# A perceiver block with a mixture of experts on one core: the clears of the dispatch buffer one at a time, and two blocks' weights behind the rows

## The reference

```python
x = x + xattn(layernorm(x), ctx, ctx)    # 16 heads, queries from x, keys and values from ctx
x = x + mamba(layernorm(x))              # see below
x = x + moe(layernorm(x))

# mamba: project to 1024 channels, conv of 4 taps, silu, then for each of 16 states
h = exp(delta_t * A) * h + delta_t * B_t * x_t
y_t = sum_over_states(h * C_t) + D * x_t

# moe: 16 experts, grouped routing (2 of 4 groups, then 4 experts a token)
act = silu(x @ gate.T) * (x @ up.T)      # 512 -> 256
y = sum_over_chosen(weight * (act @ down.T))
```

## Time and profile before

| | |
|---|---|
| runs | 1340.01, 1334.44, 1340.54 us; median 1340.01 |
| profiled execution | 1334.18 us, of which the span of the trace is 1332.2 |
| busy share of the span | PE 86%, DVE 66%, ACT 47%, POOL 10% |
| DMA | 266.27 MB, mean 200 GB/s; 58.20 MB of it in POOL's queue |
| clears | 38 of 1024 KB and 2 of 768 KB, issued from 84.9 to 312.4 us |

### The profile page before, as it was taken

The page is one execution under the profiler, slowest core; times in us unless marked ns, Lnnn a source line. Parts: engine busy times, 40 slices in busy tenths (PEclk is TensorE's granted clock), DMA queues, the critical chain, the costliest instruction groups (busy, mean ns, idle before and its releaser), DMA issues.

```text
span 1332.2 us, 13289 instructions
## 1 busy us (share of the span) xinstructions
PE 1143.1 (86%) x4276; PEld 729.0 (55%) x4276; DVE 881.5 (66%) x946; ACT 621.5 (47%) x1366; POOL 134.0 (10%) x113
## 2 busy tenths in 40 slices
PE   6988769789797899998889989629999999999992
PEld 4875646566564567675557757324444445444451
DVE  1311579666757999967799995877999974224312
ACT  4542665435355655537556635624455422222321
POOL 0010003201000043000007000030000000233002
PEclk9998889989998999999899999759999998999997
DMA  8375006998601145340035331068999984999994
GB/s 281 111 245 194 4 17 221 404 396 326 223 9 16 33 125 175 78 145 0 17 72 150 119 123 44 0 225 274 360 357 351 375 316 152 375 357 406 410 382 126
DMA packets 115188, 266.27 MB, mean 200 GB/s; under 512 B 11280, under 2 KB 44208, under 8 KB 115120
## 3 DMA queue, kind: packets, MB, share of 16 engines
q1 hardware_dynamic: 99248, 207.22, 45.1%
q0 software_dynamic: 15872, 58.20, 11.1%
HBM read 197.07 MB, written 68.32 MB: 199 GB/s over the span
## 4 chain that ended last, share of the span: by engine, by line
PE 46%; DVE 35%; DMA 8%; ACT 7%; issue 3%; POOL 1%; SPq 0%; POOLq 0%; DVEq 0%; ACTq 0%
DVE state L1348 12%; PE bank L815 9%; PE bank L776 7%; DVE state L1345 6%; PE bank L683 5%; PE bank L695 4%; PE bank L836 4%; PE bank L716 4%; DVE decay L1352 3%; DMA ctx<-in_ctx_t 3%; DVE state L1355 3%; DVE y_acc L1359 2%; PE bank L632 2%; DMA bc_bcast<-bc_scratch 2%; PE bank L747 2%
## 5 line engine op out<-in xcount | busy, mean ns | idle before, releaser
L1348 DVE TENSOR_TENSOR_SCAN state<-decay,state 128x2048 f32<-128x2048 f32 x64 | 282.9, 4421 | 23.5 <-ACT decay L1102 22.6
L815 PE MATMUL bank<-expert_w,block_x_t 128*128 128x512 f32 x496 | 227.0, 601 | 1.8 <-ACT block_x_t L1154 1.7
L683 PE MATMUL bank<-decay,params 128*128 128x512 f32 x384 | 173.3, 595 | 5.9 <-DVE decay L1352 5.9
L1639 POOL DMA_INDIRECT dispatched<-ffn_x,slot x32 | 73.0, 2280 | 756.3 <-DVE slot L1441 747.7
L1102 ACT ACTIVATE decay<-delta_even,params 128x256 f32<-128x256 f32 x256 | 107.2, 498 | 82.7 <-PE bank L683 74.2
L815 PEld LDWEIGHTS bank<-expert_w,block_x_t 128*128 128x128 f32 x496 | 91.6, 195 | 93.7 <-issue 91.6
L695 PE MATMUL bank<-ctx,queries_ctx 128*128 128x256 f32 x512 | 125.6, 403 | 16.2 <-DMA ctx<-in_ctx_t 15.0
L716 PE MATMUL bank<-probs,ctx 128*128 128x256 f32 x512 | 121.2, 392 | 11.1 <-ACT probs L1009 6.4
L1102 ACT ACTIVATE decay<-delta_odd,params 128x256 f32<-128x256 f32 x256 | 106.2, 499 | 34.5 <-PE bank L683 24.9
L695 PEld LDWEIGHTS bank<-ctx,queries_ctx 128*128 128x128 f32 x512 | 102.1, 204 | 34.2 <-DMA ctx<-in_ctx_t 16.4
L1496 DVE SCALAR_TENSOR_TENSOR hidden<-hidden,bank 128x256 f32<-128x256 f32 x62 | 26.1, 421 | 142.7 <-ACT hidden L1158 141.7
(11 more groups left out here) (193 smaller groups left out, 1334.2 us busy)
## 6 DMA issues: line engine op xcount, KB each, us to landing
dispatched<-ffn_x POOLq DMA_DIRECT2D x38, 1024.0 KB, 27.2
expert_w<-in_eg_t SPq DMA_DIRECT2D x62, 512.0 KB, 6.4
expert_w<-in_eu_t SPq DMA_DIRECT2D x62, 512.0 KB, 9.6
expert_w<-in_ed_t SPq DMA_DIRECT2D x62, 512.0 KB, 9.6
ctx<-in_ctx_t SPq DMA_DIRECT2D x32, 512.0 KB, 7.5
ctx<-in_ctx_n SPq DMA_DIRECT2D x32, 512.0 KB, 4.1
bc_bcast<-bc_scratch SPq DMA_DIRECT2D x64, 256.0 KB, 5.8
block_x<-dispatched SPq DMA_DIRECT2D x62, 256.0 KB, 9.0
```

The costliest lines, as they stand in the source:

```text
L683: mm = pe.matmul(y_bank[c][:, :], ident, dA[(g * NS + j) % NDEC][:, c * 512:(c + 1) * 512], start=False, stop=(j == NS - 1))
L815: mm = pe.matmul(o, xbT[q % 2][:, c, :], w_gu[q % NW][:, :, c, :], start=(c == 0), stop=(c == DC - 1))
L1348: dve.tensor_tensor_scan(h, dA[n % NDEC][:, 0:sw], h, 0.0, ALU.mult, ALU.add).then_inc(scan_rd, 1)
L1639: pool.indirect_dma_start(xd[WAVE_OF[c]], bass.IndirectOffsetOnAxis(slot[:, i:i + 1].bitcast(U32), 0), fx[:, t, :], None).then_inc(dispatc ...
```

## The change

In POOL's program the first clear waits for `s_full` to reach 8, and every other one for the landing of the one before it. In SP's program of wave 0 the weights of block 0 alone are issued ahead of the three `load_block_x`; those of blocks 1 and 2 come behind them.

```diff
-CLEAR_UNITS = range(8, 16)
+CLEAR_FROM = 8
...
                 if w == 0:
-                    for j in range(NW):
+                    load_gate_up(w, 0)
+                    load_down(w, 0)
+                    for j in range(NX):
+                        load_block_x(w, j)
+                    for j in range(1, NW):
                         load_gate_up(w, j)
                         load_down(w, j)
-                    for j in range(NX):
-                        load_block_x(w, j)
                     load_bc((NGR - 1) * NS + 3)
...
             pool.wait_ge(zero_rdy, 1)
+            pool.wait_ge(s_full, CLEAR_FROM)
             for i, (w, first, end) in enumerate(CLEARS):
-                n = CLEAR_UNITS[i * len(CLEAR_UNITS) // len(CLEARS)]
-                pool.wait_ge(s_full, n)
+                if i:
+                    pool.wait_ge(cleared, 16 * i)
                 v = xd[w][first:end].rearrange("(p r) d -> p r d", p=P)
```

## The result

| | before | after |
|---|---|---|
| median of the runs, us | 1340.1 (6 runs, 1334.44 to 1341.49) | 1299.61 (6 runs) |
| ratio, 95% interval | | 0.9727 [0.9686, 0.9768] |
| profiled execution, span, us | 1334.18, 1332.2 | 1305.11, 1303.2 |
| granted clock over the span | 0.941 | 0.943 |

Five of the six timings of the kernel after lie between 1293.49 and 1305.11 us; one of 2430.91 us stands apart from every other run and is left out of the ratio (without it the median is 1299.41). The kernel is 2.3 to 3.1% faster. The change adds two lines ahead of the group code and one more in POOL's part, so L695 is now L697, L716 L718, L776 L778, L1273 L1275, L1294 L1296, L1496 L1498, and the clears' L1630 is L1633.

What follows compares the result with a forecast made beforehand. No engine was busy throughout; queued clears filling the DMA engines delayed group 1's loads. Terms -5.4 + 1.5 - 20.8 + 0 - 3.1 = -27.8 us took the profiled 1334.2 to 1306.4, or 1312 on the median's scale; range 1300 to 1327.

Steps and rivals of the forecast that it cites:

- Group 0's last context load: End of group 0: with one clear ahead instead of five, PE's wait for `ctx_n` and slower matmuls go, -5.4 us.
- Group 0's projection weights: Group 0's projection: one or two clears now fall into the `in_dt_t` load, making it late, +1.5 us.
- Group 1's units: First score matmuls to `add_tiles` in group 1: falls to group 2's pace, less 2 us of remaining waits, -20.8 us.
- residual `ctx_t` waits: Group 1's units: single clears still make some `ctx_t` loads late, 2 us put on it, from 0 to 10.
- the yardstick: Group 2's 111.1 us for the same work, against group 1's 133.9, taken as the measure of a 22.8 us loss.
- Group 1's projection weights: Group 1's projection: loaded beside the last clears before and beside one clear at a time now, 0 us.
- The hole: DVE's 14.2 us stop before the first `hidden`: last scatter lands sooner, -3.1 us; the moved loads cost 0.
- The step from the profiled execution to the median: Kernel before's median lay 5.8 us above its profiled run; the same was added to 1306.4, giving 1312.
- A: At `ffn_norm(0)`: clears end too late and DVE stands, for instance 19 us, giving 1331; chance 0.1.
- B: In the units: one clear always in flight still makes every `ctx_t` load late, giving 1323; chance 0.2.
- C: Group 1: DVE's scans, not the loads, set its end, so nothing changes measurably, 1340; chance 0.05.
- D: Before the expert blocks: `gate_up(1)` late by over 4 us, 1316 instead of 1312; with the forecast, chance 0.65.

Runs made afterwards that it cites:

- e3: e1 with the chain of single clears begun at unit nine instead of unit eight: 1368.39 us, ratio 1.0209.
- e1: Kernel after with wave 0's weight loads as before, so the clears' edit alone: 1301.18 us, ratio 0.9747.
- e7: Kernel after with the fourth block's rows loaded right behind block 1's gate_up, ahead of the remaining weights: 1298.72 us, ratio 0.9744.
- e9: e7 with the sixth clear waiting for group 0's projection weights to land and the 34th for group 1's: 1293.7 us, ratio 0.9672.
- e6: e1 with the sixth clear waiting for group 0's projection weights to land and the 35th for group 1's: 1301.35 us, ratio 0.9758.
- e8: e7 with the sixth clear waiting for group 0's projection weights, and two clears in flight from the seventh on: 1300.21 us, ratio 0.9714.
- e4: e1 with all 40 clears issued from unit eight without any wait between them: 1313.15 us, ratio 0.9833.
- e5: e1 with each clear waiting for the last but one, so two in flight: 1304.24 us, ratio 0.976.
- b2: The kernel before, unchanged, profiled once more: 1339.35 us.
- a2: The kernel after, unchanged, profiled once more: 1305.5 us.
- e2: Kernel before with only the new order of wave 0's first loads, clears as before: 1337.5 us, ratio 0.998.

## Why the prediction was right, and where it was off

The sign, the cause and the place were right. The forecast of 1312 was 12 us too high against the median of 1299.61, which lies 0.4 below the range's low end (by the ratio, 0.9727 of 1340.1, it is 1303.5, inside); against the profiled execution it said 1306.4 and 1305.11 was measured.

1. **Group 0's last context load, -5.4.** It was -5.4: the stop of 4.62 us is gone and the sixteen matmuls take 3.72 us again.
2. **Group 0's projection weights, +1.5.** Near nothing. From `add_tiles(0)` to the first projection matmul it is 11.09 us in the kernel after, 11.05 before and in e3, which has no clear there, and 11.4 in e1 and e7. The clear issued at 110.82 took 11.1 us to land, so it was the clear that gave way as much as the weights. The 1.3 us more in this stretch come later in it. Of the kernels that pause the clears there e9 has them too (94.9), e6 and e8 have less (94.2 and 94.1), so the term itself is neither confirmed nor priced.
3. **Group 1's units, -20.8.** This is the term that was mis-sized: -27.0. Its mechanism held (no `ctx_t` stop, `bc_bcast` 3.4 us). The 2 us of residual `ctx_t` waits did not come: one clear in flight never made PE wait for `ctx_t` in e1, the kernel after or e3. And the yardstick was too long. Group 2's 111.1 us, from the earlier trace rows, was read as the pace without clears plus routing, but e9 does the same group with its routing in 106.3 at a clock of 1.00. Of the 111.1 some 5 us thus went with the clock, and group 1 without clears (e4) takes 105.1. The 2 us for routing were read from a window that began 7 us ahead of group 2's units: over the units alone DVE is busy 105.3 us there, not 112.5, against 101.2, and at a clock of 1.00 the two groups differ by 1.2 us (106.3 and 105.1). One step was missing: comparing the granted clock of the yardstick's window with full speed and not only with that of the stretch it is held against.
4. **Group 1's projection weights, 0.** They cost +3.7. The prediction set "beside the last clears before" equal to "one clear at a time now". The row is 10.7 us where no clear is left (e4, e5, e8), 12.3 in the kernel before and 15.0 to 17.0 with a chain of single clears, because two of its clears meet these loads: the one in flight when SP issues them at 311.02 (issued at 307.55, it lands at 312.6) and the one issued next, at 312.82.
5. **The hole, -3.1 with the moved loads at 0.** The near side was right (-3.9, DVE's stop 10.3 us where near 11 was named). The far side was not. That block 3's rows "come about 1 us late, within the same 4 us" was the step that failed. The row of the fourth block leaves SP 9.8 us after the first three and DVE loses 3.0 us. The prediction looked for the loss at `gate_up(1)`, which is 0.4 us late; it came one block later, at the rows.

The sum of the terms was -27.8 and the pair of profiles gave -29.1, since the errors of terms 3 and 4 and 5 cancel in part; so close a hit is in part luck. **The step from the profiled execution to the median, +5.8, failed.** It carried the place of the profiled run among the runs of the kernel before over to the new kernel, but there the profiled run is the slowest of the five and lies 5.5 us above the median. On the side of the kernel before one reason shows: that profile held the short version of group 1 (133.9 us, against 141.8 and 142.0 in two others) and was the fastest of its runs. With group 1 at 141.9 term 3 would be -35 and the pair -37, inside the ratio's -31 to -42 us. Group 1 is not all of it, though. The second pair of profiles, b2 and a2, differs by 33.9 us, as the last stretch of b2 is 6.8 us shorter, and why both profiles of the kernel after (1305.11 and 1305.5) lie above its other runs is not shown. What a chain of single clears does remove is group 1's own spread: its units took 106.7 to 107.1 us in all seven profiles with one.

The rivals. A (the chain ends too late) did not come, and e3 shows that it is real and priced right. The pace came out as forecast: 21 clears issued by 203 us, the rest 7.6 us apart (7.5 was taken), the last landing at 349.8 (346). For the first 21 that is partly luck: with nothing beside them they are 4.8 us apart, not 5.4, and slower ones beside the projection weights and from 174 us on made up for it. B (every `ctx_t` late by one clear in flight) is refuted for one clear; with two, e8 shows some late `ctx_t` loads, not every one. C (nothing changes) is out. D was named for `gate_up(1)` and is not what happened.

On the two rules of the Trainium skill: its page "DMA: Bandwidth & Descriptors" (Anatomy of one DMA) gives, as an estimate, 4.4 us for a clear, and a quiet one here lands after 4.5. Beside loads it is up to 13.0 us, so 261 us for the last landing was 89 us too early. The Trainium skill's page "SBUF — State Buffer" (The "DVE blocks DMA" trap) would have stretched the issues; here all forty took between 706 and 936 ns, with DVE busy for 101 of 107 us in group 1, so for these plain copies no run shows it. The scatters do vary beside DVE: in the kernel before they were issued in some 0.95 us beside its short routing operations and in 1.94, 4.08 and 2.09 us beside the 2.3 to 4.4 us operations of a scan step. Whether the port of that rule is behind it is not shown.

**What stays open.** Why the untouched stretches vary by 3 to 8 us was not found. In group 2's units the granted clock goes with the length (106.3 us at 1.00 in e2 and e9, 109.6 to 111.1 at 0.97), and roughly in the last stretch too (406.1 us at 0.98, 414.1 at 0.96). Over the whole stretch to `ffn_norm(2)` it does not: 427.8 and 436.1 us both stand beside 0.96 (e3, e5). Of the 13 timings of the kernel before beside e1, three lie between 1322.9 and 1326.6 us, far below the rest, and no profile caught such a run. Why POOL stood in e4 after 31 clears is open as well. And whether the hole's edit, with or without e7's mend, is worth anything in the time could not be told: 3 us is less than a measurement of this kernel resolves.

## What to carry to other kernels

Background copies that share the DMA engines with loads on the critical path are best started as early as their data allows (24 of 36 us here) and kept at one in flight (the other 12): in this kernel a long queue is what made loads late. The chain must still be over before the first instruction that waits for all of it. Such a chain can be paused ahead of the one large load that is needed at once, counting the copy already in flight as well; here that took 3 to 4 us off the way to group 1's projection, and e6 shows nothing of it in the time. When a load is moved behind others, look past the first consumer to each later load in the same queue, and when one group serves as the yardstick for another, read its granted clock first.

## What the runs showed that was not expected

- The cost of a clear depends on what runs beside it more than on its bytes: 4.5 us in the quiet, 5.6 to 12.4 beside group 1's unit loads in the kernel after, 11.1 and 13.0 beside the two loads of 2 MB. By the packets' own records a clear's first packet moves 1.3 us after the issue in the quiet and, in the kernel after, up to 5.1 us after it beside loads, so part of the time is a late start.
- Against the 105.1 us of group 1's units with no clear beside them (e4), one in flight costs 1.6 to 2.0 us, two in flight for the first 52 us 8.0 (e8) but for the first 28 us only 1.7 (e5), and the queue of the kernel before 29 to 37: far from in proportion.
- Where PE had stood for loads (group 1 before), the same 128 score matmuls took 5.1 us longer in all, with a granted clock of 0.95 instead of 0.98 over the stretch; the context matmuls took 29.0 us in both.
- POOL did not issue a 32nd clear behind a full queue: in the kernel before it stood 34.0 us after the 31st (issued at 272.63, the next at 307.38), in e4 79.1 us, and in both no packet of the 31 was left to move by then.
